# Five waits between GpSimd's gathers of table rows in the token stage

## What is computed

```
outs = [_level(x, idx, W, b, p, GP) for idx, W, b, p in Ws]   # p = 1, 2, 4
outs = [outs[0]] + [_interp_linear(o, n_tokens) for o in outs[1:]]
y = jnp.concatenate(outs, axis=-1)
return y @ Wf.T + bf
```

## Time and profile before

| | |
|---|---|
| median of 3 runs | 1083.06 us (1082.98 to 1085.27) |
| profiled execution | 1086.5 us |
| its span, first to last instruction | 1084.7 us |
| mean granted TensorE clock | 0.742 of 2.4 GHz |
| busy: PE, DVE, ACT, POOL | 66%, 68%, 59%, 32% of the span |

### The profile page before, as it was taken

One profiled execution on the slowest core, in us unless ns is written; L12 is line 12 of the kernel. 1 busy time (PEld: TensorE's weight loads), 2 busy tenths in 40 slices (PEclk: granted clock), 3 DMA queues, 4 the chain that ended last, 5 costly groups with the idle time before them and its releaser, 6 DMA issues. The chain is left out here.

```text
span 1084.7 us, 19299 instructions
## 1 busy us (share of the span) xinstructions
PE 712.0 (66%) x6945; PEld 525.5 (48%) x6946; DVE 737.0 (68%) x1429; ACT 643.3 (59%) x1170; POOL 346.5 (32%) x261
## 2 busy tenths in 40 slices
PE   2167647144189522119999839685787589899985
PEld 1136414022067412118999725332455348799984
DVE  3017799999888888994444446497888987344443
ACT  1015695699968554525555528765995473566664
POOL 6700064000000000025777633376000301277764
PEclk9558855555589865558999978855556699899999
DMA  3001368000055103843333354546000761133332
GB/s 100 10 1 32 108 189 252 11 8 15 0 205 166 39 0 110 288 146 73 59 61 55 45 157 178 197 172 245 4 2 1 268 256 55 42 55 58 58 46 33
DMA packets 61591, 103.12 MB, mean 95 GB/s; under 512 B 9646, under 2 KB 43586, under 8 KB 61522
## 3 DMA queue, kind: packets, MB, share of 16 engines
q1 hardware_dynamic: 45138, 85.67, 23.5%
q0 software_dynamic: 16384, 16.53, 10.0%
HBM read 74.29 MB, written 27.87 MB: 94 GB/s over the span
## 5 line engine op out<-in xcount | busy, mean ns | idle before, releaser
L2026 PE MATMUL m_pu<-m_xgT,m_w 128*128 128x256 f16 (+1 forms) x1380 | 140.9, 262 | 2.7 <-DVE m_xgT L2149 2.6
L2026 PEld LDWEIGHTS m_pu<-m_xgT,m_w 128*128 x1380 | 119.7, 100 | 17.6 <-DVE m_xgT L2149 3.5
L2045 PE MATMUL m_py<-m_w,m_hT 128*128 x1404 | 126.0, 247 | 2.8 <-issue 1.5
L2045 PEld LDWEIGHTS m_py<-m_w,m_hT 128*128 128x128 f16 x1404 | 117.0, 98 | 4.1 <-issue 2.4
L2149 DVE COPY m_xgT<-m_px 128x768 f16<-128x768 f16 (+1 forms) x46 | 22.9, 497 | 125.3 <-PE m_px L1994 125.3
L2116 ACT ACTIVATE m_pu<-m_pu,m_b,m_unit 128x256 f32<-128x256 f32 (+1 forms) x138 | 63.4, 507 | 60.3 <-PE m_pu L2026 57.8
L970 ACT ACTIVATE a_ex<-a_v,a_nb 128x256 bf16<-128x256 f16 x192 | 94.3, 493 | 5.4 <-DVE a_nb L996 5.4
L2157 DVE SCALAR_TENSOR_TENSOR m_hT<-m_pu,m_unit,m_hT 128x512 f16<-128x512 f32 (+1 forms) x138 | 86.3, 663 | 15.6 <-ACT m_hT L2109 15.1
L807 PE MATMUL a_pp<-a_room 16*128 16x256 bf16 x240 | 56.1, 412 | 39.8 <-DVE a_v L984 31.9
L2109 ACT ACTIVATE m_hT<-m_pu,m_unit 128x512 f16<-128x512 f32 (+1 forms) x138 | 81.4, 634 | 0.0
L1960 POOL DMA_INDIRECT m_xg<-xn_d,m_token x70 | 69.8, 997 | 34.7 <-issue 20.3
(11 more groups left out here) (440 smaller groups left out, 1697.2 us busy)
## 6 DMA issues: line engine op xcount, KB each, us to landing
a_room<-in_m_w SPq DMA_DIRECT2D x8, 768.0 KB, 4.4
m_stage<-in_m_w SPq DMA_DIRECT2D x8, 768.0 KB, 5.1
hv_raw<-in_m_w SPq DMA_DIRECT2D x8, 768.0 KB, 7.3
w1h_d<-hv_parts SPq DMA_DIRECT2D x8, 768.0 KB, 4.0
m_w<-w1h_d SPq DMA_DIRECT2D x8, 768.0 KB, 8.8
a_room<-in_m_w SPq DMA_DIRECT2D x8, 576.0 KB, 3.8
m_stage<-in_m_w SPq DMA_DIRECT2D x8, 576.0 KB, 5.3
hv_raw<-in_m_w SPq DMA_DIRECT2D x8, 576.0 KB, 6.3
```

The lines of the kernel that those rows point to most:

```text
L2026: last = nc.tensor.matmul(pu[:, u, q // 2, (q % 2) * w:(q % 2 + 1) * w], w1_bytes[:, bass.ds(e * (2 * W) + up_place(wpart, tail, q), 2 * P ...
L2045: last = nc.tensor.matmul(py[:, j * D:(j + 1) * D], hT[:, u, hpart, q * w + j * P:q * w + (j + 1) * P], w2_bytes[:, bass.ds(e * (2 * FC * ...
```

## The change

A dictionary names five places in the series of 32 gathers from `p0`, counted over both halves. Ahead of the gather with that number GpSimd waits for a semaphore of TensorE's. Nothing else is changed: no instruction is removed, and the order of the gathers stays.

```
+                HOLDS = {6: (turned, 4), 10: (summed, 2), 18: (mixed, 4), 24: (based, 8), 28: (turned, 6)}
                 for half in range(2):
                     for j in range(GP):
+                        if half * GP + j in HOLDS:
+                            pool.wait_ge(*HOLDS[half * GP + j])
                         pool.indirect_dma_start(g0[:, half, j, :], None, a["p0"], bass.IndirectOffsetOnAxis(
                             ap=idx0[:, half, j:j + 1], axis=0)).then_inc(gathered0[half], 16)
```

## The result

| | before | after |
|---|---|---|
| median (4 runs each) | 1084.16 us (1082.98 to 1085.66) | 1054.45 us (1052.92 to 1056.09) |
| profiled execution | 1086.5 us | 1053.25 us |
| its span | 1084.7 us | 1051.5 us |

The changed kernel takes 0.9718 of the time of the one before (95% interval 0.9684 to 0.9752), 29.7 us less by the medians. The prediction was 1056.6. The profile before was taken of one more execution, which is why its 1086.5 us lie outside the range of the four.

The account below looks back on a forecast made before the run. Neither an engine nor transfers but TensorE updates held back by GpSimd's gathers were taken to bound the token stage. 31.6 - 2.1 - 3.0 = 26.5 us off 1086.5 gave 1060.0, or 1056.6 allowing for the profiled execution; range 1043 to 1085.

Parts of the forecast that it names:

- The reading: Token stage, 23.9 to 56.3 us and 6.7 more: GpSimd's unbroken gathers hold back TensorE's updates, up to 27.9 us late.
- same: Rival: gathers are not the cause, TensorE's updates are late for a reason of its own; time 1083, chance 0.12.
- First burst: Six gathers from 16.41 us, then a wait: `turned` 4 seen at 25.15 us instead of 30.78.
- d: Delay from a burst's end until TensorE's update is seen; bounded by 0 and 6.7 us, taken as 1.3.
- Second burst: Four gathers ahead of the mixes: VectorE sees `summed` 2 at 31.45 us instead of 63.03, gain 31.6 us.
- Burst beside the mixes: Eight gathers, 10 us beside mixes of 12.8 us at half clock; held updates come in time, cost 0.
- Burst beside the interpolation: Six gathers, 8.8 us with d beside an interpolation of 7.7; cost between 0 and 4.2 us, taken as 2.1.
- Last bursts: Bursts of 4 and 4 beside the first pixels, acting as one of 11.3 us with d; cost taken as 3.0 us.
- Sum: Whole kernel: 31.6 - 2.1 - 3.0 = 26.5 us, passed on whole; 1060.0 profiled, 1056.6 expected.
- the signs: Timeline: first pause 1 to 2 us, line 665 before 31, 667 at 29 to 34, 603 near 60, "remote" waits under 10.
- Given back: Rival: later bursts hold updates in mixes, interpolation and first pixels, returning part of the gain; 1067 to 1080 us, chance 0.15.
- Slower: Rival: each pause costs d = 6.7 us and everything in a burst is held; 1086 to 1097 us, chance 0.16.

Follow-up runs that it names:

- e2: Kernel before with one wait only, for `turned` 4, ahead of the first gather from p0; 1070.73 us, 0.988 of before.
- e3: Kernel before with one wait only, ahead of the 7th gather, for the gathers' own landing instead of TensorE; 1074.96 us, 0.9912 of before.
- e5: Kernel before with a small memset and a wait for it ahead of each gather from p0, no wait for TensorE; 1057.59 us, 0.9733 of before.
- e7: Kernel before with the 32 gathers from p0 replaced by 32 plain SyncE DMAs of the same shape, in table order; 1047.01 us, one run.
- e1: Changed kernel with only the first of its five waits (`turned` 4, ahead of the 7th gather); 1070.89 us, 0.9857 of before.
- e8: Kernel before with three waits instead of five: ahead of gathers numbered 3 (`turned` 4), 10 (`mixed` 4) and 22 (`normed` 2); 1064.59 us, 0.9801 of before.
- e6: Kernel before with 32 GpSimd memsets of nearly 1 us each put ahead of the gathers from p0; 1082.18 us, one run.
- e4: Kernel before with one wait only, for `turned` 4, ahead of the 13th gather instead of the 7th; 1085.39 us, 1.0014 of before.
- e11: Same as e10 but with memsets of 128 values instead of 384; third chip, 1049.97 us, 1.0065 of before there.
- e10: Kernel before with one wait (`turned` 4, fourth gather) and a 384-value memset and wait ahead of each gather from the 16th; third chip, 1055.94 us, 1.0114 of before.
- e9: Kernel of e1 with 16 further small TensorE products behind level 2's; third chip, 1047.81 us, one run.

## Why the prediction was right, point by point

**The reading was right where the effect exists.** Gathers in a row hold back TensorE's updates, and a pause lets them out. e2 showed it from one side (no gathers, no delay), e3 from another (a pause for something else helps too), e5 from a third (spacing is enough). The rival "same", a delay of TensorE's own, is refuted on those chips. (e7, with other DMAs and no delay, says the same.) But on the third chip the outcome was that rival's, no difference, by a mechanism that I had not listed: the delay itself is absent. The prediction did not say that the effect might hang on the chip.

**First burst**: d was 2.67 us (26.54 after 23.87) and not 1.3, so `turned` 4 was seen at 26.5 instead of the expected 25.15. The step that read d off the last packets was wrong: in e3 the six gathers had landed by 25.4, and the update came at 26.64, 2.9 us after the sixth gather's end and again not with the packets.

**Second burst**: I had `summed` 2 wait for the burst's end and seen at 31.45. It was seen at 29.64, as soon as it was due, two gathers into a series. Line 462 also took 2.42 us and not 3.67, as part of it ran at the upper clock (mean granted clock 0.78 over its 2.42 us, 0.50 over the 3.67 before). The first error cost 1.4 us, the others won 3.2: the mixes start 63.43 - 30.04 = 33.4 us early; the prediction had 31.6.

**Burst beside the mixes**: cost 0, as said, and the mixes ran at half clock for 12.8 us, as taken.

**Burst beside the interpolation**: from its start to the first addition of pixels it took 86.02 - 76.21 = 9.8 us before and 54.54 - 42.83 = 11.7 now, 1.9 lost; the prediction had 2.1. 0.8 of it is the interpolation's own length, at the lower mean clock. 1.1 comes of the held copies: the last two come together at 52.14, the earlier of them 1.4 us late, and the pixels' copy behind them starts at 52.90, 1.6 us after the interpolation's end instead of 0.5. The prediction had nothing for the clock, so that its 2.1 comes so near is luck in part.

**Last bursts**: from the first addition to the first normalised rows, 7.80 us before and 7.88 now: 0.1 lost where I took 3.0. That was the term furthest off. Eight gathers ran in a row there and no update was held.

**Sum**: 33.4 - 1.9 - 0.1 = 31.4 us, which is what the projection's start shows (96.13 before, 64.74 now). The prediction had 26.5. The profiled executions differ by 33.25: the token stage's lead is passed on whole, still 31.3 us at line 1650 (857.15 before, 825.87 now at line 1653), and grows to 33.4 by line 2116 (931.71 and 898.32), in a part that the change does not touch. The second half's copy at 67.36 did not wait for its rows, as predicted.

**How near the number is.** 1056.6 against 1054.45 looks better than the working was. Profile against profile the forecast was 1060.0 and 1053.25 was measured, 6.7 us less; most of that is hidden because the profiled execution lay 3.4 us above its median before and 1.2 below it after. Of the signs, lines 665 and 667 came as said (26.60, 29.64). The first pause was 2.9 us and not 1 to 2, the "remote" waits fell from 48 to 11 us and not under 10, and line 603 came at 54.54 and not near 60.

**The rivals.** "Given back" is what e1 and e2 are: the later waits left out, and 15 to 18 us of the gain returned (0.9857 and 0.988 against 0.9718). e8 gave back 9 (0.9801), but by rows that came late. "Slower" did not occur with any set of waits. Its premise was d = 6.7 for each burst; the end of a held series showed 2.3 us (e6: 85.51 after 83.25) to 6.7 (e4: 62.97 after 56.30), but the short bursts of the change built up none after the first that held an update for more than 1.4 us.

**Prompt updates and early gathers.** On the third chip line 668 starts at 23.19, 0.04 us behind line 457's end (21.22 + 1.93). So there the trace agrees with the Trainium skill, TensorE: Matmul & The Clock Gate, "The cost: per-tile semaphore tail" (an estimate of 56 ns), and on the others it does not, for the updates named. The Trainium skill, DMA: Bandwidth & Descriptors, "Rules for kernel authors", says to issue a DMA early and to wait for it late. The third chip agrees: gathers spaced there cost 0.7 and 1.1% (e11, e10). On the affected chips the measurement goes against it: issuing the gathers later, or spaced, wins 2.8% (the change) and 2.7% (e5).

**What the condition is stays open.** On the affected chips, with gathers 1.25 us apart, the first late update was due 2.7 us after line 444's start before the change, 3.0 us after line 490's start in e1, 4.2 in e2, and 4.7 us after TensorE resumed in e6; in the changed kernel the later one was due 7.9 us after line 490's start, and in e8 it was due 9.8 us after gathers and line 490 had begun together. All these first ones lie in stretches where TensorE issues short instructions densely. In the mixes, with fewer instructions a microsecond, no delay began. That would point to gathers and dense instructions of TensorE sharing something. But it was only argued, and it can't be the whole condition: e3 has updates of the mixes nearly 7 us late, once others had been held. e9, made to test it, ran where nothing is held. What is shared, and why one chip of three does not show it, is not known.

## What to carry to other kernels

When two engines wait long for an instruction that has ended by the trace, with "remote" as releaser, look at what GpSimd does beside it: a long series of indirect DMAs at full rate held TensorE's semaphore updates for up to 27.9 us here, and on one chip of three not at all. Break the series, by waits for values that the consumers need anyway, or space it; the five waits cost nothing where the effect is absent, while spacing cost 0.7 to 1.1% there. Look also at when the last gather is issued: e5, e8, e10 and e11 all had VectorE wait 4 to 11 us for the second half's rows. And compare the kernel before on more than one chip before a gain of some per cent is believed to be general.

## What the runs showed of the hardware

- An update of TensorE's can be seen up to 27.9 us after the instruction's end, while one of ScalarE's and one of VectorE's to TensorE passed in 0.05 and 0.06 us between the late ones.
- Gathers of 128 rows 1.25 us apart do this on the affected chips. 1.66 us apart, with a memset and a wait between them, they do not (e5, at most 0.6 us late). 32 memsets in a row (e6) and 32 plain DMAs of SyncE's 0.47 us apart (e7) do not either, by one run each.
- A pause of 2.8 to 2.9 us let both held updates out and was followed by 12 and 16 gathers without a late update (the changed kernel, e1); one of 1.7 us did not do for the next (e3, held 22 us). It is no rule for the series behind it: in e8 the pause was 5.0 us, and eight gathers beside line 490 were too many.
- The same program took 1038.8 to 1047.9 us on one chip and 1079.9 to 1092.0 on two others. The token stage's 42.6 us are as much as the whole difference of the medians, 42 to 44 us, so the effect can account for all of it.
